# A two-layer decoder block: tokens in two halves, with the attention of one placed between the expert products of the other

## What is computed

```python
x = _layernorm(x + _L0_attn_ref(x, ...))    # linear attention, 16 heads of 16: elu+1 features, state k^T v
x = _layernorm(x + _L0_xattn_ref(x, itok, ctx, ctx, ctx))  # "x0": 4 experts, one for each token, by token id
x = _layernorm(x + _L0_ffn_ref(x, ...))     # "f0": 8 experts for every token, weights from a sigmoid zone ("golden")
x = _layernorm(x + _L1_attn_ref(x, ...))    # "a1": causal softmax in groups of 32; heads 8..15 rolled by 16 tokens
x = _layernorm(x + _L1_xattn_ref(x, ctx, mask))  # "x1": softmax over the 256 context rows, masked
x = _layernorm(x + _L1_ffn_ref(x, ...))     # "f1": shared part (352 rows) and top 2 of 8 experts of 176 rows
```

## Time and profile before

| | us |
|---|---|
| time, median of 3 runs | 513.49 |
| lowest, highest | 511.88, 516.61 |
| profiled execution: span | 510.0 |
| median less span | 3.5 |
| PE busy | 444.7 |
| VectorE, ScalarE, GpSimd busy | 261.6, 192.2, 222.5 |

### The profile page before, as it was taken

The page is one execution under the profiler, slowest core; times in us unless marked ns, Lnnn a source line. Parts: engine busy times, 40 slices in busy tenths (PEclk is TensorE's granted clock), DMA queues, the critical chain, the costliest instruction groups (busy, mean ns, idle before and its releaser), DMA issues.

```text
span 510.0 us, 9092 instructions
## 1 busy us (share of the span) xinstructions
PE 444.7 (87%) x3514; PEld 370.9 (73%) x3514; DVE 261.6 (51%) x662; ACT 192.2 (38%) x338; POOL 222.5 (44%) x150
## 2 busy tenths in 40 slices
PE   2977699977999999999899974487999999999982
PEld 2766488966888888888777744485887778778762
DVE  2597745575563434343576568779361223223235
ACT  3131444525444333432327661142634333333320
POOL 1320256545258455535424756302243543643622
PEclk9999889997999999999999965668899999999996
DMA  8200022110001111011100101301111121021002
GB/s 262 92 22 0 1 82 64 63 62 22 41 9 55 64 62 62 0 42 42 42 1 1 45 4 24 93 3 36 37 36 38 36 73 36 36 72 36 0 1 82
DMA packets 10242, 22.68 MB, mean 44 GB/s; under 512 B 1376, under 2 KB 5216, under 8 KB 10208
## 3 DMA queue, kind: packets, MB, share of 16 engines
q1 hardware_dynamic: 10208, 22.20, 13.5%
HBM read 20.63 MB, written 1.05 MB: 43 GB/s over the span
## 4 chain that ended last, share of the span: by engine, by line
PE 68%; DVE 19%; issue 4%; POOL 3%; ACT 2%; SPq 2%; DMA 1%; POOLq 0%; DVEq 0%; ACTq 0%
PE bank L268 13%; PE bank L271 12%; PE bank L269 12%; PE bank L438 6%; PE bank L439 6%; PE bank L440 6%; DVE stats L1013 3%; DVE x_tok L1025 2%; PE bank L405 2%; POOL rstd L880 2%; PE bank L541 2%; DVE xT_lo L1042 1%; DMA mask_w<-pad_mask_dram 1%; PE bank L560 1%; PE bank L280 1%
## 5 line engine op out<-in xcount | busy, mean ns | idle before, releaser
L916 POOL TENSOR_TENSOR h_lo<-scratch,h_hi 128x512 fp32r<-128x512 f32 x76 | 98.2, 1293 | 153.6 <-ACT h_hi L750 153.6
L268 PE MATMUL bank<-xT_hi,pk_hi 128*128 128x512 f32 x272 | 112.6, 414 | 6.7 <-ACT xT_hi L686 3.9
L269 PE MATMUL bank<-xT_hi,pk_lo 128*128 128x512 f32 x272 | 109.8, 404 | 0.0
L1214 DVE TENSOR_TENSOR scratch<-bank,scratch 128x512 f32<-128x512 f32 x76 | 52.5, 691 | 106.8 <-PE bank L271 66.3
L750 ACT ACTIVATE h_hi<-scratch 128x512 fp32r<-128x512 f32 x76 | 48.1, 633 | 125.5 <-DVE scratch L1214 125.5
L438 PE MATMUL bank<-pk_hi,h_hi 128*128 128x256 f32 x304 | 86.0, 283 | 6.5 <-POOL h_lo L916 6.4
L271 PE MATMUL bank<-xT_lo,pk_hi 128*128 128x512 f32 x272 | 88.2, 404 | 0.3
L439 PE MATMUL bank<-pk_lo,h_hi 128*128 128x256 f32 x304 | 85.2, 280 | 0.0
L440 PE MATMUL bank<-pk_hi,h_lo 128*128 128x256 f32 x304 | 85.2, 280 | 0.0
L873 POOL TENSOR_TENSOR pk_lo<-pk_raw,pk_hi 128x896 fp32r<-128x896 f32 (+3 forms) x28 | 67.9, 2426 | 25.0 <-ACT pk_hi L676 24.8
L268 PEld LDWEIGHTS bank<-xT_hi,pk_hi 128*128 128x128 f32 x272 | 52.6, 194 | 22.8 <-issue 10.2
(11 more groups left out here) (203 smaller groups left out, 618.0 us busy)
## 6 DMA issues: line engine op xcount, KB each, us to landing
pk_raw<-pk_f_dram SPq DMA_DIRECT2D x14, 448.0 KB, 3.2
pk_raw<-pk_f_dram SPq DMA_DIRECT2D x8, 768.0 KB, 4.4
pk_raw<-pk_x_dram SPq DMA_DIRECT2D x4, 512.0 KB, 3.6
q_buf<-x_cols_dram SPq DMA_DIRECT2D x2, 512.0 KB, 6.0
x_tok<-x_rows_dram SPq DMA_DIRECT2D x1, 1024.0 KB, 10.3
pk_raw<-pk_x_dram SPq DMA_DIRECT2D x4, 256.0 KB, 4.4
out_dram<-x_tok SPq DMA_DIRECT2D x4, 256.0 KB, 2.2
wa_raw<-w_attn_dram SPq DMA_DIRECT2D x1, 768.0 KB, 4.7
```

Source lines behind the costliest of these rows:

```text
L268: pe.matmul(o, w(kc)[0], x(kc)[0], start=kc == 0, stop=False)
L269: pe.matmul(o, w(kc)[1], x(kc)[0], start=False, stop=False)
L916: pool.tensor_tensor(h_lo[:, h, c * 512:(c + 1) * 512], hraw[:, r, :], h_hi[:, h, c * 512:(c + 1) * 512].bitcast(F32), ALU.subtract).then_ ...
L1214: TT(hraw[:, r, :], other[:, :], sil[:, r, :], ALU.mult).then_inc(sems["hid_mul"], 1)
```

## The change

**Halves apart.** Units now run half by half: x0 with all four experts on the first half, then on the second; f0 with eight and eight; f1 with all 14 packs on the first half, then on the second. A step `s` is a chunk of a unit (two for each unit in x0 and f0, one in f1): 16 steps of x0, 32 of f0, 28 of f1, and `unit_of(s)` names the unit. Each pack of f0 and f1 is therefore loaded and split twice. An f0 pack is loaded in a gate-and-up part and a down part, in rings of their own; GpSimd takes the low part of gate and up, VectorE that of down (`d_low`), and the 128 columns that spread the combine weights get no low part. f1 has three raw slots. All sums of downs use banks 4 and 5, everything beside them banks 6 and 7. Cross weights of x1 and the weights of a1 come through a buffer of their own.

**Tables.** What isn't an expert product is cut into numbered pieces, and tables give each piece a position: 2s is after the gate of step s, 2s + 1 after its downs. Every engine has the same loop over the steps and puts its part of a piece there. In `ATTN` 0 to 2 are norm and transposes, 3 to 11 self-attention, 12 to 14 its residual and norm, 15 to 18 cross attention, 19 to 21 norm 8 or 9 and its transposes, 22 to 24 the router of f1. `GOLDEN` is the norm before f0 and its router, `FIRST` the second half's norm after a0.

**Shapes.** In self-attention two tiles are taken together; scores have 64 rows and 128 columns in place of 128 and 256 (`QH = 4` heads to a group), four masked copies of the keys in place of eight for each tile, made from the bank directly. Softmax pieces are of 1024 columns. All loops are written out; no hardware loop is left.

The core of the diff (the pieces of an engine are its functions of before, cut at the positions):

```diff
+N1 = CH_R + CH_S
...
+U_F0, U_F1 = 2 * EX, 2 * EX + 2 * E0
+S_F0, S_F1 = 2 * U_F0, 2 * U_F1
+S_END = S_F1 + 2 * N1
+W_X0, W_F0, W_X1 = KC * D, 3 * KC * D, 2 * KC * D
+G_F0, D_F0 = 2 * KC * D, KC * D
+G_F1, GLO_F1, D_F1 = 2 * D + P, 2 * D, D
...
+ATTN = ({0: 65, 1: 66, 2: 68, 3: 70, 4: 71, 5: 73, 6: 74, 7: 75, 8: 76, 9: 78, 10: 79, 11: 80, 12: 82, 13: 83, 14: 86,
+         15: 87, 16: 89, 17: 91, 18: 92, 19: 93, 20: 94, 21: 95, 22: 96, 23: 97, 24: 100},
+        {0: 96, 1: 97, 2: 99, 3: 101, 4: 102, 5: 104, 6: 105, 7: 106, 8: 107, 9: 109, 10: 111, 11: 112, 12: 114, 13: 115,
+         14: 118, 15: 119, 16: 120, 17: 121, 18: 122, 19: 123, 20: 123, 21: 123, 22: 124, 23: 125, 24: 129})
+GOLDEN = ({0: 19, 1: 21, 2: 25, 3: 33, 4: 34, 5: 35}, {0: 38, 1: 40, 2: 43, 3: 49, 4: 51, 5: 53})
+FIRST = ({}, {0: 1, 1: 3, 2: 6})
...
+def steps_at(table, pos):
+    return [(i, h) for h in range(2) for i, at in sorted(table[h].items()) if at == pos]
...
+def place(u, c):
+    return (u % 2, c) if u < U_F1 else ((u - U_F1) // 2 % 2, u % 2)
...
+LOADS = [("g", 0), ("d", 0), ("g", 1), ("d", 1), ("s", 0), ("g", 2), ("d", 2), ("g", 3)]
+for m in range(4, 2 * E0):
+    LOADS += [("g", m), ("d", m - 1)] + [("s", m // 2 - 1)] * (m in (4, 6, 8))
+LOADS += [("d", 2 * E0 - 1)]
+LOADS += [("f1", k) for k in range(2 * N1)]
+LOADS.insert(LOADS.index(("f1", 6)), ("s", 4))
+S_SLOT = {0: 17, 1: 21, 2: 25, 3: 46, 4: 50}
```

```diff
+            def gate(s):
+                u, c = unit_of(s)
+                if u < U_F0:
+                    if u < EX and c == 0:
+                        pe.wait_ge(sems["xw_lo"], u + 1)
+                elif u < U_F1:
+                    pe.wait_ge(sems["g_lo"], u - U_F0 + 1)
+                else:
+                    pe.wait_ge(sems["g_lo"], 2 * E0 + u - U_F1 + 1)
+                first = {0: 0, 2 * EX: 1, S_F0: 2, S_F0 + 2 * E0: 3, S_F1: 8, S_F1 + N1: 9}.get(s)
+                if s >= 2:
+                    pe.wait_ge(sems["hid_mul"], s - 1)
+                if u < U_F1:
+                    product(s, bank[2 * c][:, :], 0, D, c * P, first).then_inc(sems["gate_ready"], 1)
+                else:
+                    product(s, bank[(3 * (u - U_F1)) % 4][:, :], 0, P, 0, first).then_inc(sems["gate_ready"], 1)
...
+            def up(s):
+                u, c = unit_of(s)
+                if u < U_F0:
                     return
...
+                if u < U_F1:
+                    product(s, bank[2 * c + 1][:, :], KC * D, D, c * P).then_inc(sems["up_ready"], 1)
+                    return
+                m, h = u - U_F1, (u - U_F1) // N1
+                if routed(m):
+                    pe.wait_ge(sems["silu_done"], s)
+                    if m % N1 == CH_S:
+                        pe.wait_ge(sems["cwT_done"], h + 1)
+                    pe.matmul(bank[(3 * m + 1) % 4][:, :], g_part("f1", m, pk_hi)[0:2 * E1, 2 * D:2 * D + P],
+                              cwT[:, h * 512:(h + 1) * 512], start=True, stop=True).then_inc(sems["cw_ready"], 1)
+                if m and routed(m - 1):
+                    pe.wait_ge(sems["m1_done"], routed_no(m))
+                else:
+                    pe.wait_ge(sems["hid_mul"], s)
+                product(s, bank[(3 * m + 2) % 4][:, :], D, P, 0).then_inc(sems["up_ready"], 1)
...
+            for s in range(S_END):
+                u, c = unit_of(s)
+                gate(s)
+                beside(2 * s)
+                up(s)
+                if s == S_F0 + 2 * E0:
+                    down(u - 1)
+                if s == S_F1 - 1:
+                    down(u - 1)
+                    down(u)
+                elif c == 1 and u > 0 and u != U_F0 + E0:
+                    down(u - 1)
+                elif u >= U_F1 + 2:
+                    down(u - 2)
+                beside(2 * s + 1)
+            down(U_F1 + 2 * N1 - 2)
+            down(U_F1 + 2 * N1 - 1)
```

```diff
+            for s in range(S_END):
+                u, c = unit_of(s)
+                silu(s)
+                beside(2 * s)
+                hidden_high(s)
+                for kind, i in g_at(s):
+                    g_high(kind, i)
+                for i in S_SLOT:
+                    if S_SLOT[i] == s:
+                        s_high(i)
+                beside(2 * s + 1)
+                for kind, i in d_at(s):
+                    d_high(kind, i)
...
+            for s in range(S_END):
+                u, c = unit_of(s)
+                beside(2 * s)
+                hidden(s)
+                if s == S_F0 + 2 * E0:
+                    add(u - 1)
+                if s == 20:
+                    later_constants()
+                if s == S_F1 - 1:
+                    add(u - 1)
+                    add(u)
+                elif c == 1 and 0 < u < U_F1 and u != U_F0 + E0:
+                    add(u - 1)
+                beside(2 * s + 1)
+                for kind, i in d_at(s):
+                    d_low(kind, i)
+                if s == S_F1 + N1 + 1:
+                    last_add(0)
+                if s == S_F1 + N1 + 2:
+                    norm(10)
             last_add(1)
             norm(11)
```

```diff
+            for kind, i in LOADS:
+                if (kind, i) == ("d", 2 * E0 - 1):
+                    rolled(0)
+                elif (kind, i) == ("f1", 12):
+                    rolled(1)
+                elif (kind, i) == ("f1", N1 + 7):
+                    store(0)
+                load(kind, i)
+            store(1)
```

1508 lines of the change are left out of this document (784 added, 724 removed).

## The result

Four runs of each on one chip gave 528.19 us for the changed kernel (526.73 to 533.59) and 512.68 for the kernel before (511.52 to 516.61): a ratio of 1.0302, interval 1.0231 to 1.0374. It is 15.5 us slower where a gain of 32 was forecast. Medians are over all runs of a kernel; in runs 7, 14 and 15 one run of each fell into a slower state of the chip, and only the ratios and their intervals leave it out.

A forecast was written before the change was run, and what follows sets the result against it. TensorE bounds the expert stages; for 92 us it waits, then runs at half clock. Head 54.6, expert products 308.3, other work 72, waits 30 and tail 12.2 give 477.1, plus 3.5 over the profiled span: 481 us, range 463 to 500.

The forecast's parts named there:

- The frame and the work: Sum along TensorE: expert products 308.3 us at unchanged unit prices, its other work 72 us between them at full clock.
- The hole in the clock strip: The 92 us stretch around layer-1 attention where TensorE waits and runs at half clock; forecast to vanish.
- The mid-f1, f1-start and x0 waits: TensorE waits between f1's halves 5.5 us, at f1's start about 5.5, at x0's start 5.
- rival C: f1's three-slot pack ring binds because loads come twice as often: slower, 523 us; chance 0.04.
- Rival E: Interleaving doesn't happen; TensorE takes the attention in one piece: 513 to 518 us; chance 0.02.
- The head and the tail: Before the first x0 product 54.6 us, unchanged; from the last down product's wait to the end 12.2 us.
- What it adds, and who hides it: Second load and split of every pack, extra table loads: hidden by TensorE's 106 us in f1, nothing added for splits.
- the sum of waits: TensorE's waits across x0, attention steps and f1, including 3 us for lower clock: 30 us in all.
- the clock: TensorE's lower clock for a while after the long waits: 3 us.
- rival D: Table switches in attention and golden steps cost a drain too: 15 us more, 496 us; chance 0.05.
- B: More waits, since attention steps sit in four in-order queues: 501 us, or 511 with waits doubled; chance 0.15.
- The chances: Faster by over 1% 0.92, within 1% 0.04, slower 0.04; the forecast itself (470 to 492) 0.60.

The follow-up runs named there:

- run 7: Changed kernel with each half's attention and cross step in one piece, not interleaved with expert products: 592.71 us, 1.1519 of the kernel before.
- run 14: Changed kernel with each low part made once, stored to DRAM in the first half and loaded back in the second: 523.96 us, 1.0158.
- run 15: The kernel of run 14 with the order edits of run 5: 524.30 us, 1.0156 of the kernel before.
- run 10: Changed kernel with GpSimd's low parts of all f0 and f1 packs shrunk to 32 columns, result incomplete: 509.45 us, 0.9941.
- run 17: Changed kernel with GpSimd's low parts shrunk to 32 columns for only the eight packs of f0's first half, result incomplete: 518.96 us, 1.0120.
- run 6: Changed kernel with 103 needless 512-column matmuls on TensorE ahead of eight of its long waits: 524.30 us, 1.0229 of the kernel before.
- run 13: The kernel of run 12 with 48 needless 512-column matmuls ahead of six waits: 519.30 us, 1.0128 of the kernel before.
- run 8: Changed kernel with every exp and sigmoid behind the head replaced by a copy, removing 20 of 22 table loads: 522.56 us, 1.0200.
- run 5: Changed kernel with order edits together: golden weights in four parts, VectorE's low parts later, value tiles apart, some norm, split and mask positions moved: 519.77 us, 1.0124.
- run 9: The order edits of run 5 with some positions moved again and 67 needless matmuls ahead of remaining waits: 520.20 us, 1.0133.
- run 12: Changed kernel with all f0 and f1 pack low parts on VectorE, plus order edits (golden weights in four parts, value tiles apart, positions moved): 519.82 us, 1.0123.
- run 16: The kernel of run 15 with 48 needless 512-column matmuls ahead of six waits of TensorE: 520.38 us, 1.0149 of the kernel before.
- run 1: Changed kernel with VectorE's choice of the golden weights cut into four parts at four positions: 529.37 us, 1.0289 of the kernel before.
- run 4: Changed kernel with only positions moved at the two ends of the first half's attention: 528.68 us, 1.0286 of the kernel before.

## Why the prediction was wrong

**The frame and the work were right.** The work came out within 5 us. Expert units keep their price (4.83 to the 4.79 of the earlier trace rows), the rest of TensorE's work with it: 385.2 us to 380.3. The scores were 6.2 us to 6. The hole in the clock strip went. The mid-f1, f1-start and x0 waits were 6.0, 5.0 and 4.0 us to 5.5, 5.5 and 5. The pack ring (rival C) never bound: with loads twice as often the units of f1's second half are 4.83 us apart. Rival E fell by run 7.

**The head and the tail** were 3.5 us over and 0.6 under; the head's 3.5 us (2.8 in the second profile) weren't followed up.

**The step that failed first is "What it adds, and who hides it".** I priced the second split of every pack in engine time ("with eleven splits more they stay under 65. TensorE's 106 us hide that") and put nothing in the sum. Shrinking GpSimd's part gives 19 to 21 us (run 10) of the 47 to 49 that the time missed by, half of it by the eight splits beside the golden weights and the rest of f0's first half (run 17). The repeated splits alone are the smaller part: without them (run 14, with loads in their place) it was 4 to 6 us. The mechanism has two parts. While GpSimd makes a low part, VectorE's operations with two operands in SBUF stand still until it ends: 26 to 28 us of VectorE's busy time were hold by the pack splits, by run 10. And VectorE has down parts of its own, 27 us in run 10; 17 us of that hold make them the 44 of the changed kernel. The Trainium skill ("SBUF — State Buffer", section Who interferes with whom) says that the port pair which VectorE shares with GpSimd is an exclusive lock, and that a VectorE instruction with two SBUF inputs contends for it with a GpSimd instruction that reads SBUF. The trace agrees: 2.33 us beside 2.40, 3.43 beside 3.50, and 0.19 without. This rule spoke against the change, bore on a row that I quoted (2.08 us for a comparison), and I didn't weigh it. That TensorE's 106 us cover the splits said nothing: the expert multiply stands in VectorE's queue, and TensorE is only two steps ahead.

**The second is the sum of waits.** The golden weights were put at 1 us and cost 5.33 + 1.83 + 2.89 = 10.1: the string of 34 operations was costed by its place, not by what is queued behind it. The first half's attention and the end of f0 were put at 6 and cost 17.6: 3.73 by copies that came behind a held split, 4.83 by stops in the value matmuls, 4.83 at the end of f0, where the third cross pack's split (2.36) and the power of norm 8 stand on GpSimd ahead of a hidden low part. The second half's was put at 4 and cost 7.6, 4.4 of it stops. Of the stops, 9.2 us in all, had shown nothing: I took the one row of 1.26 us without a stop for all eight tiles, though the kernel before had 4.8 us of them too.

**The third is the clock, put at 3 us (4.4 with the tail) and measured at 30.** I knew that waits cost clock, but counted the kernel before as if its hole were the whole loss and short waits harmless. In the kernel before 22.2 us were lost for 36.8 waited, most of it where TensorE was waiting; at that 0.60 my own 29.2 us of waits would have lost some 17 us (an estimate), four times what I put. So about half of the clock's miss is this price, and the rest follows from the longer waits. Spread among products, a dozen waits of 1 to 5 us each are followed by several us at half clock, at full load. Run 6 shows the cause: with needless work in place of eight of the waits, lost clock fell to 13.3. Run 13 shows the limit: there the fill cost what the clock gave back.

**The table loads** (rival D, 15 us, "I count it within the softmax waits") cost 6 to 8 us (run 8). The drain of about 1380 ns that the Trainium skill ("ScalarE: Activation LUTs", section What ACT_TABLE_LOAD costs) gives showed nowhere: each load is one row of 1.283 us.

**Of the rivals, B came nearest** ("when VectorE is held by a semaphore, the expert multiply behind it is held too"), at 511 us with waits doubled. It had the queue right, but the hold was by GpSimd and not by a semaphore, and it left the clock out: with 26 us more it would have been 537. My slower cases held little because each took one mechanism alone; what came was three at once. The chances don't add either: E, at 513 to 518, belongs within 1% of before, so my own list gives 0.90 faster and 0.06 within, and not 0.92 and 0.04.

**What stays open.** No complete kernel with the halves apart came below the one before: the best took 519 to 520 us (runs 5, 9, 12, 13, 16). Runs 14 and 17 together suggest that the splits beside the first half of f0 have to go, or the golden weights have to move to where nothing is split; neither was tried in a complete kernel. Nor would that alone bring the forecast: run 10, without any of GpSimd's pack splits, still ended 28 us over 481, with 34.7 us of waits and 22.4 of lost clock. How much of run 10's gain is the hold and how much GpSimd's shorter queue is open. What makes TensorE stop among small matmuls wasn't isolated beyond their number in a row.

## What to carry to other kernels

Price a moved or doubled step in the time of the engine that it holds up and not in its own: list what each queue does in the same microseconds, and look for short operations with long rows; where such a row ends with GpSimd's, GpSimd's work is paid for in VectorE's queue too. Price the clock from the kernel at hand: here it was 0.4 to 0.65 us lost for each microsecond that TensorE waited, in every complete kernel without fills, so a forecast of waits alone is short by about a third of what they cost. And when single edits only move waits to the next place, as in runs 1 and 4, take work from the queue that the chain goes through, and there where its strings stand: sparing eight packs gave 9 to 11 us (run 17), sparing 22 elsewhere 4 to 6 (run 14).

## What the runs showed of the hardware

- Held operations: VectorE's 32-column operations took 2.33 and 3.43 us beside GpSimd's 2.40 and 3.50, and 0.19 without; the multiply of a bank by an SBUF tile wasn't held: 687 ns on average over all 76.
- Half clock also followed short pauses: after waits of 0.93 and 0.76 us at 97 to 99 us the window from 100 to 104 stood at 0.57; filling waits kept it at 1.00. Rows of 32x17 matmuls stood at 0.67 with pauses of 2.5 us in them.
- TensorE stopped for 2.1 to 2.5 us (1.5 to 2.6 in the second profile) among 256 matmuls of 32x17, after 153 to 217 of them, and for 0.7 to 1.0 among 128 with products between. No run shows why.
- 44 stores and 44 loads of 128 to 512 KB more, 59 MB in place of 36 in 520 us, took the landing of a pack from 3.3 to 3.8 us.
